# One decoder kernel: the first recurrence's order is rewritten, and TensorE sums the terms of both sequences' recurrences

## The reference, cut to what matters

```
x = x + self_attention_16_heads_of_8(norm(x))
x = x + cross_attention_8_heads_of_64(norm(x), ctx)
x = x + two_class_attention(norm(x))       # keys split by a classification of the tokens
x = x + delta_recurrence(norm(x))
x = x + cross_attention_16_heads_of_64(norm(x), ctx)
x = x + ternary_feed_forward(norm(x))

# delta_recurrence, per sequence and head (16 heads, d = 8); q, k are l2-normalised
beta = sigmoid(x @ Wbeta)
state = state * (1 - b*k_i*k_j) + b*v_i*k_j          # elementwise, step t
out_t[i] = sum_j state[i, j] * q_t[j]
out = layernorm(out) * ln_g + ln_b
out = out * silu(x @ Wg)
return out @ Wout
```

## Time and profile before

| what | us |
|---|---|
| median of 3 runs | 452.13 |
| lowest, highest | 451.67, 454.27 |
| the profiled execution's own time | 452.82 |
| its span, first to last instruction | 450.9 |
| TensorE busy in it | 372.1 (83%) |
| VectorE busy | 270.0 (60%) |
| ScalarE busy | 210.0 (47%) |
| GpSimd busy | 126.8 (28%) |

### The profile page before, as it was taken

The page is one execution under the profiler, slowest core; times in us unless marked ns, Lnnn a source line. Parts: engine busy times, 40 slices in busy tenths (PEclk is TensorE's granted clock), DMA queues, the critical chain, the costliest instruction groups (busy, mean ns, idle before and its releaser), DMA issues. The chain is left out here.

```text
span 450.9 us, 7394 instructions
## 1 busy us (share of the span) xinstructions
PE 372.1 (83%) x2791; PEld 207.1 (46%) x2791; DVE 270.0 (60%) x577; ACT 210.0 (47%) x359; POOL 126.8 (28%) x119
## 2 busy tenths in 40 slices
PE   2777788798979989778798878676888898989986
PEld 1543333344445443324355543253544454755555
DVE  3765643666656471556644686548887658468345
ACT  2354556445536432225566352233454566345634
POOL 5000000145543052000000134011685564346600
PEclk9988999999999996889999998989998999999999
DMA  7600000010000000000001000000000000000000
GB/s 208 177 1 2 0 2 1 1 48 1 0 1 2 0 2 0 0 0 3 3 2 48 0 1 0 0 2 0 1 2 0 1 1 1 2 0 1 1 2 23
DMA packets 9688, 6.16 MB, mean 14 GB/s; under 512 B 3755, under 2 KB 8758, under 8 KB 9654
## 3 DMA queue, kind: packets, MB, share of 16 engines
q1 hardware_dynamic: 9654, 5.69, 4.8%
HBM read 5.39 MB, written 0.26 MB: 13 GB/s over the span
## 5 line engine op out<-in xcount | busy, mean ns | idle before, releaser
L1258 DVE TENSOR_REDUCE mxw<-PS 128x2 f32<-128x1024 f32 x48 | 58.5, 1221 | 24.2 <-PE PS L640 23.9
L1029 ACT ACTIVATE Pc<-PS 128x1024 f32<-128x1024 f32 x48 | 49.0, 1022 | 23.1 <-PE PS L668 21.9
L554 POOL TENSOR_TENSOR Psum<-Pc 128x512 f32<-128x512 f32 x24 | 30.9, 1289 | 101.9 <-ACT Pc L1029 101.3
L1255 DVE TENSOR_REDUCE mx<-PS 128x4 f32<-128x1024 f32 x32 | 39.0, 1223 | 27.0 <-PE PS L633 26.9
L696 PE MATMUL ACC<-Pc,V 128*64 128x256 f32 x384 | 52.2, 393 | 0.0
L556 POOL TENSOR_TENSOR Psum<-Psum,Pc 128x512 f32<-128x512 f32 x22 | 27.9, 1267 | 39.2 <-ACT Pc L1029 38.9
L1029 ACT ACTIVATE Ps<-PS 128x1024 f32<-128x1024 f32 x32 | 32.7, 1022 | 12.0 <-PE PS L652 11.0
L696 PEld LDWEIGHTS ACC<-Pc,V 128*64 128x64 f32 x384 | 23.5, 136 | 24.1 <-issue 15.8
L708 PE MATMUL PS<-ones_h 128*128 128x512 f16 x122 | 30.3, 395 | 2.1 <-DVE Khl_a L1307 2.0
L568 POOL TENSOR_TENSOR mid<-mid 128x256 f32<-128x256 f32 x2 | 1.4, 725 | 100.5 <-ACT mid L1134 100.5
L557 POOL TENSOR_TENSOR Psum<-Psum,Pc 128x512 f32<-128x512 f32 x22 | 28.0, 1272 | 1.7
(11 more groups left out here) (286 smaller groups left out, 716.0 us busy)
## 6 DMA issues: line engine op xcount, KB each, us to landing
Qm<-mrow SPq DMA_DIRECT2D x64, 0.5 KB, 1.7
wq_c<-in_c_Wq_dram SPq DMA_DIRECT2D x1, 512.0 KB, 5.3
spread<-in_c_Wo_dram SPq DMA_DIRECT2D x1, 512.0 KB
Pc<-in_ctx_dram SPq DMA_DIRECT2D x1, 384.0 KB, 4.5
wk_c<-in_c_Wk_dram SPq DMA_DIRECT2D x1, 384.0 KB, 6.5
wv_c<-in_c_Wv_dram SPq DMA_DIRECT2D x1, 384.0 KB, 7.4
csth<-in_const_dram SPq DMA_DIRECT2D x1, 320.0 KB, 4.9
x<-in_x_dram SPq DMA_DIRECT2D x2, 128.0 KB, 2.4
```

Source lines behind the costliest of these rows:

```text
L554: alone(v.tensor_tensor(t, p[:, :, 0, :], p[:, :, 1, :], ALU.add), "sums_done")
L1029: e = A(to, src.rearrange("p a c -> p (a c)"), ACT.Exp, scale=PHASES[name].scale)
L1255: last = v.tensor_reduce(to, src.rearrange("p e (t s) -> p e t s", t=2), AX, ALU.max)
L1258: last = v.tensor_reduce(to, src, AX, ALU.max)
```

## The change

- V8's two memsets go from GpSimd's queue to the head of VectorE's.
- In `prep`, all eight spread matmuls are issued first, and only then, for the mixer, TensorE waits for the classes and issues the eight one-row matmuls. `start` is set on the first matmul of each bank only.
- The job dn is split in two: dn (squares' sums, beta, beta*v) and dn2 (from the root on). For sequence 0 the order dg, dn becomes dn, dn2, dg.
- GpSimd keeps one product a round and writes it to a room of its own (`d_terms`); its adds are gone. In oT, TensorE takes each term's four 128x128 blocks in fp32 against the identity and sums them all in PSUM: sixteen matmuls in place of two transposes, for both sequences. ScalarE's wait for the adds in sp goes.
- `ends` is reordered: V1[6] and V1[7] come into the first rounds, K1[4] behind the fourth, K1[5] to K1[7] later; dp, dn and dn2 of sequence 1 come forward into `ends`. Its dp waits on ScalarE for sequence 0's oT instead of its dout. K1[7] goes into `three`.
- WARM: the 18 matmuls ahead of norm 3's xt of sequence 1 go, oT of sequence 0 gets 6, yT of sequence 0 has 8 for 12, norm 4's xt of sequence 0 has 8 for 12.

```diff
@@ schedule
         -8: V1[4], -7: K1[1], -5: K1[2], -3: K1[3], 1: [qx], 3: [rs], 7: [rt], 10: [rv], 11: [zT, qx_], 12: [out, rs_] + ln, 13: ln2 + V1[5], 14: xt,
-        15: [dp, rt_], 16: [dg, dn], 18: [dt]})
-    ends = [rv_] + [s0] + K1[4] + [zT_, s1] + V1[6] + [out_] + ln_ + [s2] + K1[5] + [s3] + ln2_ + V1[7] + xt_ + [oT, dl] + K1[6] \
-        + [dl2, yT] + K1[7] + [dout] + ln4 + ln24 + xt4
+        15: [dp, rt_], 16: [dn, dn2, dg], 18: [dt]})
+    ends = [rv_, s0] + V1[6] + [zT_, s1, out_] + V1[7] + [s2] + ln_ + [s3] + K1[4] + [oT] + ln2_ + [dl] + xt_ + K1[5][:1] \
+        + [dl2, yT, dp_] + K1[5][1:] + [dout] + ln4 + K1[6][:1] + ln24 + xt4 + [dn_] + K1[6][1:] + [dn2_]
     three = attentions((y1, 0, -9, 0), (y1, 1, 13, 2))
...
-        -9: [dp], -8: [dg, dn], -5: [dt], -4: [s0], -2: [s1], 0: [s2], 2: [s3], 4: [oT], 5: [dl], 6: [dl2],
+        -8: [dg_], -5: K1[7] + [dt], -4: [s0], -2: [s1], 0: [s2], 2: [s3], 4: [oT], 5: [dl], 6: [dl2],
@@ WARM
-    job("rt", "mixer", 0): 6, job("dt", "", 0): 16, job("xt", "", 1, 3): 18, job("yT", "", 0): 12, job("xt", "", 0, 4): 12,
+    job("rt", "mixer", 0): 6, job("dt", "", 0): 16, job("oT"): 6, job("yT", "", 0): 8, job("xt", "", 0, 4): 8,
@@ decoder
-        d_acc = wq2["cross0"]
+        d_terms = [wq2["cross0"][:], d_kq, d_kbv, d_q[1]]
@@ GpSimd
-            alone(v.memset(V8, 0.0), "pool_set")
-            alone(v.memset(V8.rearrange("p t h c -> p (t h) c")[:, :, 8:9], 1.0), "v8_set")
...
-                    if u == 0:
-                        if b == 1:
-                            after(pool, "oT")
-                        alone(v.tensor_tensor(d_acc[:], d_st, q_, ALU.mult), "d_prod")
-                    else:
-                        alone(v.tensor_tensor(q_, d_st, q_, ALU.mult), "d_prod")
-                        alone(v.tensor_tensor(d_acc[:], d_acc[:], q_, ALU.add), "d_added")
-                    if u == 3:
-                        alone(v.tensor_tensor(d_acc[:, 0:S], d_acc[:, 0:S], d_acc[:, S:2 * S], ALU.add), "d_sum")
+                    if u == 0 and b == 1:
+                        after(pool, "oT")
+                    alone(v.tensor_tensor(d_terms[u], d_st, q_, ALU.mult), "d_prod")
@@ TensorE, prep
+                    dst = take(j)
+                    for X, w in enumerate((spread_k, spread_q)):
+                        for uu in range(2):
+                            to, unit = dst[:, X, uu * S:(uu + 1) * S], slice((2 * u + uu) * P, (2 * u + uu + 1) * P)
+                            mm(to, w["h"][:, unit], hl16[:, b, 0, X * S:(X + 1) * S], start=(uu == 0), stop=False)
+                            last = mm(to, w["l"][:, unit], hl16[:, b, 1, X * S:(X + 1) * S], start=False, stop=not classes and uu == 1)
                     if classes:
                         pe.wait_ge(sem("cls_done"), 1)
                         pe.wait_ge(sem("csth_in"), 16)
-                    dst = take(j)
...
+                        for X, rows in enumerate((cls_k, cls_q)):
+                            for uu in range(2):
                                 for c, r in enumerate((R_POS, R_NEG)):
...
@@ TensorE, oT
-                    pe.wait_ge(sem("d_sum"), b + 1)
-                    dst = take(j)
-                    turn_tokens(dst[:, 0, :], lambda t: d_acc[:, t * P:(t + 1) * P]).then_inc(sem("ring"), 1)
+                    for m in range(4):
+                        pe.wait_ge(sem("d_prod"), 4 * b + m + 1)
+                        if m == 0:
+                            dst = take(j)
+                        for e in range(2):
+                            for t in range(2):
+                                last = mm(dst[:, 0, t * P:(t + 1) * P], d_terms[m][:, e * S + t * P:e * S + (t + 1) * P], ident,
+                                          start=(m == 0 and e == 0 and t == 0), stop=(m == 3 and e == 1 and t == 1))
+                    last.then_inc(sem("ring"), 1)
@@ ScalarE
                     if b == 1:
-                        after(act, "dout")
+                        after(act, "oT")
...
-                    if u >= 3:
-                        act.wait_ge(sem("d_added"), 3 * b + u - 2)
@@ VectorE
+            then(v.memset(V8, 0.0))
+            v.memset(V8.rearrange("p t h c -> p (t h) c")[:, :, 8:9], 1.0).then_inc(sem("v8_set"), 1)
             for j in plan:
...
+                elif kind == "dn2":
...
                     dve.wait_ge(sem("d_root"), b + 1)
```

More of the change, by code:

```diff
@@ L197, in schedule @@
     zT_, out_ = small_tail(f0, 1)
[L198 removed]
+    dp, dg, dn, dn2, dt, s0, s1, s2, s3, oT, dl, dl2, yT, dout = delta(0)[3:]
+    dp_, dg_, dn_, dn2_ = delta(1)[3:7]
     place_in(two, {
         -8: V1[4], -7: K1[1], -5: K1[2], -3: K1[3], 1: [qx], 3: [rs], 7: [rt], 10: [rv], 11: [zT, qx_], 12: [out, rs_] + ln, 13: ln2 + V1[5], 14: xt,
[L201 to L203 removed]
+        15: [dp, rt_], 16: [dn, dn2, dg], 18: [dt]})
+    ends = [rv_, s0] + V1[6] + [zT_, s1, out_] + V1[7] + [s2] + ln_ + [s3] + K1[4] + [oT] + ln2_ + [dl] + xt_ + K1[5][:1] \
+        + [dl2, yT, dp_] + K1[5][1:] + [dout] + ln4 + K1[6][:1] + ln24 + xt4 + [dn_] + K1[6][1:] + [dn2_]
     three = attentions((y1, 0, -9, 0), (y1, 1, 13, 2))
[L206 removed]
+    dt, s0, s1, s2, s3, oT, dl, dl2, yT, dout = delta(1)[7:]
     (ln, ln2, xt), (ln_, ln2_, xt_) = norm(4, 1), norm(5, 0)
@@ L773, in _ @@
                         pe.wait_ge(sem("csth_in"), 16)
-                    dst = take(j)
-                    for X, (w, rows) in enumerate(((spread_k, cls_k), (spread_q, cls_q))):
-                        for uu in range(2):
-                            to, unit = dst[:, X, uu * S:(uu + 1) * S], slice((2 * u + uu) * P, (2 * u + uu + 1) * P)
-                            mm(to, w["h"][:, unit], hl16[:, b, 0, X * S:(X + 1) * S], start=True, stop=False)
-                            last = mm(to, w["l"][:, unit], hl16[:, b, 1, X * S:(X + 1) * S], start=False, stop=not classes)
-                            if classes:
+                        for X, rows in enumerate((cls_k, cls_q)):
+                            for uu in range(2):
                                 for c, r in enumerate((R_POS, R_NEG)):
-                                    last = mm(to, csth[0:1, r:r + P], rows[0:1, c, b, :], start=False, stop=(c == 1))
+                                    last = mm(dst[:, X, uu * S:(uu + 1) * S], csth[0:1, r:r + P], rows[0:1, c, b, :],
+                                              start=False, stop=(uu == 1 and c == 1))
                     last.then_inc(sem("ring"), 1)
@@ L1401, in _ @@
                         .then_inc(sem("dve_side"), 1)
+                elif kind == "dn2":
+                    heads = lambda r: r.rearrange("p (a d) -> p a d", d=8)
+                    over = lambda r, n: r.unsqueeze(2).to_broadcast([P, n, 8])
                     dve.wait_ge(sem("d_root"), b + 1)
```

4 lines of the change are left out of this document (1 added, 3 removed).

## The result

The change makes the kernel faster: 435.88 us (median of four runs, 433.86 to 438.26) against 452.49 for the kernel before (four runs beside them, 451.67 to 454.27). The ratio is 0.963, with a 95% interval of 0.9566 to 0.9693: 16.6 us gone where 12.4 were forecast. The profiled execution of the new kernel is the fastest of its four, 433.86, with a span of 432.1 (before: 450.9 and 452.82).

A forecast was written before the change was run, and what follows sets the result against it. TensorE was taken to lead by far, with engines taking turns in sequence 0's recurrence. Terms 1.1 + 2.7 + 9.1 - 0.5 = 12.4 us off the 452.1 median gave 439.7, range 433 to 446.7.

The forecast's parts named there:

- the rival in which the clock holds: Stretches from 172 and 343 us also stay at 2.4 GHz, 3.4 and 1.3 us more: 435 us, chance 0.17.
- The start: V8's memset on VectorE frees line 1220, so line 1231 ends sooner: gain 1.1 us, bounds 0.7 and 1.3.
- The classes: Preps: spread matmuls fill the first prep's wait, 1.7 us; fewer changes of kind in three others, 1.0; sum 2.7.
- the half-rate stretch: Eight 512-column passes behind the first prep at 1.2 GHz; 3.4 us if it went, left out for the range.
- Sequence 0: Six steps from dt to sequence 1's dt, summing to a gain of 9.1 us, bounds 5 and 12.
- the rounds: Sequence 0's four rounds, first spread matmul to last scan: 17.45 us becomes 16.2, gain 1.3, bounds 0 and 2.4.
- the terms: Sequence 0 behind the last scan: one GpSimd product and four fp32 matmuls; gain 2.2 us, with TensorE waiting 2.0.
- to yT: Sequence 0, stretch to yT: no K2 queued on VectorE's path any more; gain 3.3 us.
- to dt of sequence 1: From norm 4's xt: dt's banks wait for the last K2, then twelve fillers take 2.7 us; gain 0.2.
- the waits move: New TensorE standstills of 2.0 and 2.5 us drop the clock, sequence 1 nearly unrepaid: 446.7 us, chance 0.15.
- Doing the projection early buys nearly nothing: Sequence 1's projection brought forward gains little, since dt waits for a K2; that stretch gains 0.2 us.
- Sequence 1: Sixteen fp32 matmuls add 3.6 us, mostly regained from waits and shorter scans: loss 0.5, bounds loss 3.6, gain 2.

The follow-up runs named there:

- experiment 2: Kernel before with only prep's new order (spread matmuls first, then the wait for the classes): 441.31 us against 451.98, ratio 0.9781.
- experiment 4: Kernel before with 22 idle matmuls for 14 ahead of the first prep, prep's order left: 449.07 us against 452.08, ratio 0.9946.
- experiment 5: Kernel before with prep's matmuls grouped by kind, but the wait for the classes still ahead of all sixteen: 447.8 us against 451.09, ratio 0.992.
- experiment 3: New kernel with prep's old order of matmuls (wait for the classes first, kinds mixed): 443.22 us against 451.65, ratio 0.9819.
- experiment 8: New kernel with dp, dn and dn2 of sequence 1 back in their old place, list three: 432.84 us against 451.98, ratio 0.959.
- experiment 9: New kernel with K1[7] and its K2 moved from ahead of sequence 1's dt to behind the first spread: 434.43 us against 451.65, ratio 0.9625.
- experiment 11: New kernel with sequence 1's dp, dn, dn2 back in list three, dn and dn2 ahead of dg, K1[7] behind the first spread: 434.79 us, ratio 0.9624.
- experiment 12: New kernel with sequence 1's dt and first spread directly behind dg, K1[7] after them, four fillers for twelve: 438.95 us against 452.08, ratio 0.9728.
- experiment 6: New kernel, but GpSimd adds the terms for both sequences and TensorE only transposes: 438.04 us against 452.08, ratio 0.9695.
- experiment 7: New kernel, but GpSimd adds the terms for sequence 1 only, TensorE only transposing there: 436.89 us against 451.98, ratio 0.9681.
- experiment 10: New kernel without the twelve idle matmuls ahead of sequence 1's dt: 433.97 us against 451.65, ratio 0.9613.

## Why the prediction was right in direction and short in size

The direction and the order of size held, and the time was 3.8 us below the forecast. Of the cases it was between the forecast (own range 436 to 443) and the rival in which the clock holds (435, chance 0.17), and by its mechanism it was that rival: the stretches from 172 and from 343 us both went.

**The start.** Forecast 1.1, measured 1.27, by the steps told: line 1220 freed (0.47 at 5.05; 0.25 near 5.2 was forecast), line 1231 unstretched beside the memset of mxw. The agreement in size is partly luck. Three other kernels leave V8 on GpSimd (experiments 2, 4 and 5), and in their traces the statistics of x's second tile began 0.2 to 0.3 us sooner, line 1220 began ahead of the long memset, and line 1231 met it instead. This is experiment 4:

```profile
5.01 1.81 POOL L532 MEMSET small_kv<- 128x2048 f32 x1
...
5.57 1.40 DVE L1231 TENSOR_SCALAR xn<-x,mv,rstd 128x128 f32<-128x128 f32 x2
```

The norm that follows was scaled at 12.24 to 12.36 in these three, at 13.12 in the kernel before, and at 11.39 to 12.11 in the ten kernels with the memset on VectorE. Against the three the move is worth about 0.5 us on average, and the rest of the 1.27 is the late start of the one execution that both the forecast and the table are read from. Another 0.9 came between 15 and 36 us, where TensorE's clock rises sooner (eight matmuls of 256 columns take 1.05 from 15.43, in the kernel before 1.75 from 16.69) and a later stretch at half rate is missing. The norm ahead of the class attention comes at 152.5 to 155.5 in the ten kernels (mean 154.2) and at 154.3 to 156.1 in the four that leave the memset on GpSimd (mean 155.4). So of the 2.18 that the table has there, about 1.2 is the edit's by these averages and 1.0 is luck. On the Trainium skill's figure (VectorE: DVE Perf Modes, "Zero memsets can be issued as uint32"), an estimate of 2.1, the measured 1.76 is shorter; the memset began at 1.22, not at about 0.7 as forecast, so the first statistics still came 0.10 later than before. The Trainium skill's rule on who locks whom (SBUF — State Buffer, "Who interferes with whom") holds for line 1231 beside the long memset: 1.40 to 1.53 in those three traces for 0.60. Beside the memset of mxw no run shows it for that line: it took its usual 0.60 from 5.97 in the new kernel, 0.12 before that memset's end, and from 7.24 in the kernel before, 0.37 before it. So the 0.3 that the prediction had by the rule did not appear, and its reading that line 1231 does not bear the rule out holds for that memset only.

**The classes: the step that failed.** The forecast was 1.7 at the first prep and 1.0 for the three others; measured in the timelines 1.87 and, by experiment 5, about 1.1 for the three others by grouping. Both terms were right. What was mis-sized is the term set to 0 beside them, the half-rate stretch (3.4, "I leave it out and keep it for the range"), and 3.4 would have been too small: the second prep's step is 3.84, about 3.3 of it clock, and some 1.3 more of clock follows by dp's copy, 4.6 together. From the norm to dp's copy the kernel gains 7.57, for 2.7. The argument against it, that the one-row matmuls behind the wait are short, had no row. The standstill ahead of the prep goes with the clock: with 1.65 it falls (experiments 3 and 5, in either order of matmuls), with 0.63 or none it holds (the new kernel, experiments 2 and 4), but for experiment 8's execution. A standstill does not always do it either: behind the wait of 2.12 ahead of the last term the new kernel's next four key matmuls, at 263.80, take 1.88, the full rate.

**Sequence 0.** 9.1 forecast, 8.8 measured, and step by step: dt 1.1 and 1.3; the rounds 1.3 and 1.6; the terms 2.2 and 2.0, with the TensorE wait of 2.0 measured as 2.12; to yT 3.3 and 3.5, of which experiment 2 gets 1.35 by the clock alone; to norm 4 1.0 and 1.7; to dt of sequence 1 a gain of 0.2 and a loss of 1.4. That last one has the right cause and a wrong size: the fillers begin at the end of K2, as was said, but they take 4.13, not 2.7, because the first of them run at half rate behind the wait of 2.54. The forecast had that wait and that clock in a rival ("the waits move") and not in the step. "Doing the projection early buys nearly nothing" held (experiment 8), and so did its reason (experiments 9 and 11: wherever dt goes, that K2 stands in the way; experiment 12: past it, the second round waits instead).

**Sequence 1.** A loss of 0.5 forecast, 0.3 gained. The lag came as told, 2.1 at oT's copy, and all of it came back, half of it by the gate's product (the wait of 2.12 is now 1.49) and half with the clock behind 338 us, which had been left out with the other. The second half comes without this edit as well (experiments 2 and 6), so the edit itself lost 0.9, near the forecast's 0.5, and the sign of the measured 0.3 is the clock's. What would have shown the forecast wrong, a lag that never comes back, did not happen. By experiment 7 the edit for this sequence can't be told from no effect.

**The sum.** 2.2 (start, with the accident) + 7.6 + 8.8 + 0.3 = 18.9 in the profiled execution, and 16.6 in the medians; the difference is that the profiled execution was the fastest of four. About 1.0 of the 2.2 at the start is luck, as said above. Against the forecast: classes 4.9 more, the start 1.1 more, sequence 1 0.8 more, sequence 0 0.3 less, and 2.3 less for the median.

**What stays open.** Why filling one wait at 169 us also removes the slices at 0.8 behind 271 us in experiment 2, where neither an order nor a wait was edited, while experiment 5 keeps two of the three. The work there meets the clock at another moment; no run isolates that. Whether experiment 8 (0.959) or 10 (0.9613) truly beats the new kernel (0.963) isn't settled: intervals of half a per cent each way overlap. Both traces say that the idle matmuls behind the 2.54 wait are the weak place.

## What to carry to other kernels

Where TensorE stands still for a microsecond or more and a rise and fall of the granted clock follows, price the work behind it at both levels and take the clock as a case of its own, not as a remainder for the range: here it was 4.4 of the 7.3 us at the preps, while the removed wait itself was 1.1. Work that doesn't need the awaited value belongs ahead of the wait, and matmuls of one kind together, since a change of kind costs on its own. Look at several profiled executions before a difference of a microsecond at one place is called an effect: here the start of one of them was late by chance. Before bringing a chain forward, look up which buffer its next step takes and who frees that last; here the same K2 stood ahead of dt or of the first spread in the new kernel and in experiments 9 and 11.

## What the runs showed of the hardware

- A change of kind between 128-row and one-row matmuls costs: eight of one-row in a row take 1.04, four groups of two spread and two one-row take 2.57 (180.56 to 183.13), grouped 1.95 (173.29 to 175.24), so about 0.1 for each change saved. The edit also sets `start` on fewer matmuls; no run parts the two.
- Idle matmuls that start behind a wait of 2.54 us raise the clock only at their own price: twelve take 4.13, some 1.4 more than at full rate (2.75 in experiment 8), for transposes in 1.04. Without them the transposes take 1.94 (experiment 10): 0.9 lost for 4.1 saved, of which 3.1 arrive at the first scan.
- VectorE clears 2048 fp32 columns in 1.76 us, 0.86 ns a column, as fast as GpSimd's 1.80.
- While GpSimd clears those 2048 columns, a VectorE tensor_scalar on fp32 data that begins meanwhile ends only with the memset or behind it: 1.69 for two columns, 1.40 to 1.53 for two tiles of 128 columns that take 0.60 alone (experiments 2, 4 and 5). Which one is hit depends on when x arrives.
- Within one kernel the time goes with the mean granted clock, about 1 us for 0.003 to 0.004 (0.988 and 433.9, 0.973 and 438.3). Kernels that differ by less than 2 us need more than four runs each.
